# Row maxima of the first and last attention turned by a transposing transfer instead of TensorE: once and twice per batch, written as fp16, with the keys' constant row at minus one

## The reference

```python
# block 0
h = _ln(x) * (1 + sc_msa) + sh_msa
x = x + _self_attn(h) * g_msa           # windows of 128 rows, rolled by 64       -> group "w"
h = _ln(x) * (1 + sc_mca) + sh_mca
x = x + _topk_cross_attn(h, ctx) * g_mca  # top 16 of 256 keys                    -> group "t"
h = _ln(x) * (1 + sc_mlp) + sh_mlp
x = x + _swiglu(h) * g_mlp              # hidden size 1024
# block 1
scores = einsum('bqhd,bkhd->bhqk', q, k) / sqrt(16)
x = x + (einsum('bhqk,bhkd->bqhd', softmax(scores), v) @ Wp + bp)  # 256 x 256    -> group "l"
```

## Time and profile before

| | us |
|---|---|
| median of 3 runs | 1281.58 |
| the profiled execution: its own time | 1281.51 |
| its span, first to last instruction | 1279.6 |
| PE busy (matmul, ends modelled) | 1197.1 |
| DVE busy | 1128.0 |
| ACT busy | 1035.5 |
| POOL busy | 852.7 |
| granted TensorE clock, mean | 0.988 |

### The profile page before, as it was taken

The page is one execution under the profiler, slowest core; times in us unless marked ns, Lnnn a source line. Parts: engine busy times, 40 slices in busy tenths (PEclk is TensorE's granted clock), DMA queues, the critical chain, the costliest instruction groups (busy, mean ns, idle before and its releaser), DMA issues. The chain is left out here.

```text
span 1279.6 us, 39100 instructions
## 1 busy us (share of the span) xinstructions
PE 1197.1 (94%) x13710; PEld 850.3 (66%) x13710; DVE 1128.0 (88%) x3808; ACT 1035.5 (81%) x2193; POOL 852.7 (67%) x1134
## 2 busy tenths in 40 slices
PE   7778898999999999999999999999999999989887
PEld 6665566667676776767676766767676766656654
DVE  3579999899999999999999999999999999988443
ACT  3745688889897979889897989889797979776864
POOL 1315597959586877868686877968596877857310
PEclk9989999999999999999999999999999999999999
DMA  7531021211111121212021121212021121110111
GB/s 200 157 81 43 23 76 34 61 38 45 48 50 54 47 64 27 55 44 73 27 68 44 47 64 52 51 27 64 15 81 30 47 56 42 28 27 2 43 35 34
DMA packets 111392, 67.27 MB, mean 53 GB/s; under 512 B 13836, under 2 KB 107870, under 8 KB 111198
## 3 DMA queue, kind: packets, MB, share of 16 engines
q1 hardware_dynamic: 109166, 63.71, 18.8%
q10 hardware_dynamic: 2032, 1.05, 0.5%
HBM read 22.33 MB, written 4.19 MB: 21 GB/s over the span
## 5 line engine op out<-in xcount | busy, mean ns | idle before, releaser
L1246 ACT ACTIVATE prob<-turned_score 128x1024 f32<-128x1024 f32 x320 | 325.7, 1018 | 82.8 <-PE turned_score L908 81.2
L1521 POOL TENSOR_TENSOR pair<-full,pair 128x512 f16<-128x512 f32 x182 | 210.6, 1162 | 112.8 <-ACT pair L1201 106.6
L1405 DVE MATCH_REPLACE8 rest<-top,score 128x256 f32<-128x256 f32 x512 | 208.2, 415 | 0.0
L1419 DVE MATCH_REPLACE8 far<-best,rest 128x256 bf16<-128x256 f32 x512 | 205.7, 409 | 0.5 <-issue 0.5
L1402 DVE MAX8 top<-score 128x8 f32<-128x256 f32 x512 | 193.4, 419 | 10.7 <-PE score L908 10.3
L1527 POOL TENSOR_SCALAR far<-far 128x512 bf16<-128x512 bf16 x256 | 158.6, 620 | 61.9 <-DVE far L1419 42.6
L1392 DVE TENSOR_REDUCE rowmax_l<-score 128x4 f32<-128x1024 f32 x121 | 147.6, 1220 | 30.5 <-issue 19.8
L908 PE MATMUL work<-pair_n,w_m_hi 128*128 128x256 f16 x1024 | 173.6, 273 | 0.3 <-issue 0.3
L908 PE MATMUL work<-pair_n,w_m_lo 128*128 128x256 f16 x512 | 139.5, 273 | 0.0
L1201 ACT ACTIVATE pair<-full 128x512 f16<-128x512 f32 x192 | 121.0, 630 | 18.0 <-ACT full L1194 0.7
L908 PEld LDWEIGHTS work<-pair_n,w_m_hi 128*128 128x128 f16 x1024 | 96.2, 98 | 20.0 <-issue 9.5
(11 more groups left out here) (212 smaller groups left out, 3191.0 us busy)
## 6 DMA issues: line engine op xcount, KB each, us to landing
k_stack_t<-pair SPq DMA_DIRECT2D x96, 64.0 KB, 2.5
k_stack_l<-pair SPq DMA_DIRECT2D x96, 64.0 KB, 2.6
q_stack_w<-pair SPq DMA_DIRECT2D x93, 64.0 KB, 2.6
k_stack_w<-pair SPq DMA_DIRECT2D x93, 64.0 KB, 2.6
q_stack_t<-pair SPq DMA_DIRECT2D x93, 64.0 KB, 2.6
q_stack_l<-pair SPq DMA_DIRECT2D x93, 64.0 KB, 2.6
ctx_t<-in_ctx_turned SPq DMA_DIRECT2D x16, 256.0 KB, 2.9
ctx_l<-in_ctx SPq DMA_DIRECT2D x16, 256.0 KB, 2.8
```

The source lines that it names most:

```text
L1246: act.activation(prob[:, at:at + 2, :], both_b[:, :, :], ACT.Exp).then_inc(exp_done, 1)
L1405: m = dve.match_replace(rest[p % 2][:, t, :], eight[:, t, :], bank[:, t * L:(t + 1) * L], -FAR)
L1419: m = dve.match_replace(far[p % NFAR][:, t, :], best[p % 2][:, t, :], rest[p % 2][:, t, :], -FAR)
L1521: pool.tensor_tensor(pr[:, 1, :, :], whole[:, :, :], pr[:, 0, :, :], ALU.subtract).then_inc(split_lo, 1)
```

## The change

Groups w and l get their guards another way, except the first batch of w and the last batch of l, which keep the old way (`EDGE_GUARDS`). `rm` writes its maxima as fp16 into a 128x128 tile `rowmax_*`, zeroed once at the start by POOL; w has one such tile, filled by all 4 `rm` of a batch, l has two, each filled by 4 of 8. A new SP piece `gx` waits for the last of these `rm`, turns the whole tile with a transposing transfer from SBUF to SBUF (`turned_max_*`), and `gg`, waiting for it, sends the used rows into the query stack: 32 rows once for w, 16 rows twice for l. `gd` (PE) and `gc` (ACT) go. The top-16 group keeps its four guards per batch.

The maxima are no longer negated by ACT. Instead the keys' constant row is minus one. The same tile of constants multiplied the last projection's bias, so that bias is negated too.

Counts over the whole program: PE's `gd` falls from 192 to 72, ACT's `gc` likewise; SP has 45 `gx` more, and `gg` falls from 192 to 117. All five order lists and the places of the idle matmuls are written anew; the idle matmuls go from 518 to 627.

```diff
+GUARDS = {"w": 1, "t": 4, "l": 2}
+EDGE_GUARDS = {("w", 0): 4, ("l", 15): 4}
...
-IDLE_WORK = ("pj_wq:0:0=59 a_w:0:0=6 gd_w:0:0=22 gd_w:0:1=19 gd_w:0:2=11 bk_w:0:0=17 x4_n2:0:0=25 pj_tq:0:0=38 "
...
+IDLE_WORK = ("pj_wq:0:0=59 wp:0:6=14 gd_w:0:0=19 gd_w:0:2=11 pr_w:0:0=37 x4_n2:0:0=11 pj_tq:0:0=38 a_w:1:0=21 "
...
-        rowmax = {s: [sb(f"rowmax_{s}{i}", [P, 8], F32) for i in range(2)] for s in "wl"}
-        guard = {s: [sb(f"guard_{s}{i}", [8, P], F16) for i in range(2)] for s in "wtl"}
+        edge_rowmax = [sb(f"edge_rowmax{i}", [P, 8], F32) for i in range(2)]
+        rowmax = {s: [sb(f"rowmax_{s}{i}", [P, P], F16) for i in range(GUARDS[s])] for s in "wl"}
+        turned_max = {s: sb(f"turned_max_{s}", [P, P], F16) for s in "wl"}
...
+                elif kind == "gx":
+                    each = (8 if s == "w" else 16) // groups(s, b)
+                    sp.wait_ge(a_free, a_unit(s, b, each * (i + 1) - 1))
+                    if guard_no(s, b, i) > 0:
+                        sp.wait_ge(guard_in[s], 16 * guard_no(s, b, i))
+                    sp.dma_start(turned_max[s][:, :], rowmax[s][i][:, :], transpose=True).then_inc(rowmax_turned[s], 16)
+                elif kind == "gg" and by_transfer(s, b):
+                    many = H // 2 // groups(s, b)
+                    sp.wait_ge(rowmax_turned[s], 16 * (turned_no(s, b, i) + 1))
+                    sp.dma_start(stack[s][b % NS[s]]["q"][NR:64 + NR + 1:64, many * i:many * (i + 1), :],
+                                 turned_max[s][0:4 * many, :]).then_inc(guard_in[s], 16)
...
-                    pe.wait_ge(guard_in[s], 16 * (NG * b + (i if s == "w" else i // 2) + 1))
+                    pe.wait_ge(guard_in[s], 16 * (guard_no(s, b, i * groups(s, b) // (4 if s == "w" else 8)) + 1))
...
-            dve.memset(ones[:, :], 1.0).then_inc(ones_set, 1)
+            dve.memset(minus_ones[:, :], -1.0).then_inc(ones_set, 1)
...
+                    if by_transfer(s, b):
+                        dve.wait_ge(rowmax_zeroed, 1)
+                        if i % each == 0 and turned_no(s, b, g) >= GUARDS[s]:
+                            dve.wait_ge(rowmax_turned[s], 16 * (turned_no(s, b, g) - GUARDS[s] + 1))
+                        maxima = rowmax[s][g]
...
             pool.memset(minus_half[:, :], -0.5)
+            for s in "wl":
+                for one in rowmax[s]:
+                    m = pool.memset(one[:, :], 0.0)
+            m.then_inc(rowmax_zeroed, 1)
```

More of the change, by code:

```diff
@@ L54, with groups, by_transfer, turned_no @@
 BY_TWO = {"wk": 0, "wq": 0, "tq": 0, "lq": 15}
+GUARDS = {"w": 1, "t": 4, "l": 2}
+EDGE_GUARDS = {("w", 0): 4, ("l", 15): 4}
+def groups(s, b):
+    return EDGE_GUARDS.get((s, b), GUARDS[s])
+def by_transfer(s, b):
+    return s != "t" and (s, b) not in EDGE_GUARDS
+def turned_no(s, b, g):
+    return sum(groups(s, one) for one in range(b) if by_transfer(s, one)) + g
+def guard_no(s, b, g):
+    return sum(groups(s, one) for one in range(b)) + g
 ORDERS = {
     "pe": (
[129 rows of a table removed]
-    "act": (
[100 rows of a table removed]
-    "dve": (
[70 rows of a table removed]
-    "pool": (
[88 rows of a table removed]
-}
-IDLE_WORK = ("pj_wq:0:0=59 a_w:0:0=6 gd_w:0:0=22 gd_w:0:1=19 gd_w:0:2=11 bk_w:0:0=17 x4_n2:0:0=25 pj_tq:0:0=38 "
-             "a_w:1:0=13 a_t:0:0=20 b_w:1:0=28 o_w:1:0=8 a_t:0:2=9 a_t:0:5=61 x4_n2:1:0=14 b_t:0:4=16 a_t:1:0=11 "
-             "pr_w:2:0=12 x4_n4:14:0=5 o_l:13:2=12 ot_l:13:0=10 bk_l:13:0=8 m2:15:2=11 x4_n4:15:0=5 pj_lq:15:0=19 "
-             "a_l:15:7=12 bk_l:15:0=14 pr_l:15:0=33")
[118 rows of a table added]
+    "act": (
[89 rows of a table added]
+    "dve": (
[70 rows of a table added]
+    "pool": (
[85 rows of a table added]
+}
+IDLE_WORK = ("pj_wq:0:0=59 wp:0:6=14 gd_w:0:0=19 gd_w:0:2=11 pr_w:0:0=37 x4_n2:0:0=11 pj_tq:0:0=38 a_w:1:0=21 "
+             "a_t:0:0=20 a_w:1:2=14 a_w:1:3=32 a_t:0:1=25 a_t:0:2=11 gd_t:0:0=26 bk_w:1:0=28 pr_w:1:0=22 "
+             "x4_n2:1:0=43 a_t:0:7=5 o_t:0:3=6 bk_t:0:0=19 b_w:2:0=17 pr_w:2:0=5 x4_n3:15:0=43 xt_m:15:0=8 "
+             "x4_n4:15:0=10 a_l:14:7=19 a_l:15:1=10 o_l:14:3=7 bk_l:15:0=14 pr_l:15:0=33")
 def idle_work():
@@ L538, in build @@
         half_bias = sb("half_bias", [P, HC], F32)
-        ones = sb("ones", [33, L], F16)
+        minus_ones = sb("minus_ones", [33, L], F16)
         last_bias = sb("last_bias", [33, C], F16)
@@ L668, in build @@
         guard_out = {s: sem(f"guard_out_{s}") for s in "wtl"}
+        rowmax_zeroed = sem("rowmax_zeroed")
+        rowmax_turned = {s: sem(f"rowmax_turned_{s}") for s in "wl"}
         stat_done = {s: sem(f"stat_{s}") for s in LN if s not in SUMMED}
@@ L757, in unit, with guard_before @@
             return i // 2, i % 2
+        def guard_before(n, s):
+            b = max(one for one in range(B) if guard_no(s, one, 0) <= n)
+            return d_no["gd_" + s, b, n - guard_no(s, b, 0)]
         def heads(g):
@@ L850, in _ @@
                             for one in stack[group]:
-                                sp.dma_start(one["k"][NR:64 + NR + 1:64, :, :], ones[0:H, :]).then_inc(filled, 16)
+                                sp.dma_start(one["k"][NR:64 + NR + 1:64, :, :], minus_ones[0:H, :]).then_inc(filled, 16)
                     if load_no[i] >= NSTAGE:
@@ L1012, in _ @@
                     else:
-                        src = rowmax[s][n % 2][:, :]
-                    turn(d_take(piece, b, i)[0:8, 0:P], src).then_inc(d_ready, 1)
+                        src = edge_rowmax[n % 2][:, 0:rows]
+                    turn(d_take(piece, b, i)[0:rows, 0:P], src).then_inc(d_ready, 1)
                 elif kind == "b":
@@ L1098, in _ @@
                                        k == 0 and n == 0, False)
-                            m = mm(bank[:, t * C:(t + 1) * C], ones[:, 0:P], last_bias[:, :], False, True)
+                            m = mm(bank[:, t * C:(t + 1) * C], minus_ones[:, 0:P], last_bias[:, :], False, True)
                         m.then_inc(d_ready, 1)
@@ L1234, in _ @@
                         act.wait_ge(guard_in[s], 16 * (n - 1))
-                    act.activation(guard[s][n % 2][:, :], d_bank("gd_" + s, b, i)[0:8, 0:P], ACT.Copy,
-                                   scale=-1.0).then_inc(guard_out[s], 1)
+                    act.activation(guard[s][n % 2][0:rows, :], d_bank("gd_" + s, b, i)[0:rows, 0:P], ACT.Copy).then_inc(guard_out[s], 1)
                 elif kind == "e":
@@ L1377, in _ @@
                 elif kind == "rm":
-                    n = NG * b + (i if s == "w" else i // 2)
+                    each = (4 if s == "w" else 8) // groups(s, b)
+                    g, n, half = i // each, guard_no(s, b, i // each), H // groups(s, b)
                     if (s, b, i) not in by_bank_no:
                         dve.wait_ge(a_ready, a_no["a_" + s, b, i])
-                    if n >= 2 and (s == "w" or i % 2 == 0):
-                        dve.wait_ge(d_ready, d_no["gd_" + s, (n - 2) // NG, (n - 2) % NG])
-                    at, wide, of = (0, 4, P) if s == "w" else (2 * (i % 2), 2, L)
+                    if by_transfer(s, b):
[3 more added lines that the diff above has]
+                        maxima = rowmax[s][g]
+                    else:
+                        if i % each == 0 and g >= 2:
+                            dve.wait_ge(d_ready, d_no["gd_" + s, b, g - 2])
+                        maxima = edge_rowmax[n % 2]
+                    at, wide, of = (4 * (i % each), 4, P) if s == "w" else (2 * (i % each), 2, L)
                     if (s, b, i) in by_bank_no:
```

30 lines of the change are left out of this document (16 added, 14 removed), and 747 rows, old and new, of the table ORDERS.

## The result

The changed kernel takes 1304.95 us (median of 4 runs, 1300.71 to 1308.24), the kernel before 1282.62 beside it. The ratio is 1.018 with a 95% interval of 1.016 to 1.020. I had predicted 1271 us and a range of 1257 to 1292. Sign and range are both wrong.

A forecast was written before the change was run, and what follows sets the result against it. The prediction took DVE and PE to share the limit, with PE's list giving way. Turns -19.2, lateness of w +4.5 and DVE order +4.4 made -10.3 us against 1281.51, so 1271 us, range 1257 to 1292.

The forecast's parts named there:

- turns: On PE, 120 turns of w and l go at 0.16 us each: 19.2 us won, counted in full.
- guard of w late: On PE at w's first turned piece: transfers take 5.3 us against 5.0 of cover, 15 times, 4.5 us lost.
- order of DVE: On DVE, 50 places instead of 42 where it waits for PE to refill score banks: 4.4 us lost.
- A microsecond that leaves it lets DVE start that much earlier: Steady stretch: time taken off PE's list passes to DVE in full, until 22.5 us of DVE's waits are used up.
- It is covered: New wait of l: 16 to 24 us of PE matmuls in batches 0 to 11 cover the 5.3 us chain; no cost.
- I count nothing for SP: On SP, 75 guard transfers go, 45 transposing ones come, SP standing still for their landing: counted as no cost.
- rival 4: SP, standing still 45 times for 3 us, delivers top-16 guards late: 13 us against 10.3 won, 1285 us; chance 0.05.
- 1: Rival: the transposing transfer outlasts its cover at PE's first turned piece of w, 15 batches: 1298 us; chance 0.22.
- 2: Rival: DVE is the bound and no PE time passes through: 1279 to 1284 us; chance 0.14.
- 3: Rival: all goes through, 25 us from turns, 5 from PE's waits for maxima, no lateness: 1256 us; chance 0.14.

The follow-up runs named there:

- e5: Kernel before, old lists, without the guards of w and l except in their edge batches, maxima not subtracted there: 1271.8 us, ratio 0.991.
- e15: Kernel before with each of the 120 turns of w and l made three times in a row into the same bank: 1298.2 us, ratio 1.012.
- after: The changed kernel itself, with new lists and transposing transfers for the guards of w and l, against the kernel before: 1304.95 us, ratio 1.018.
- e13: Changed kernel without the guards of w from batch 1 on, l keeping its 30 transposing transfers: 1303.4 us, ratio 1.017.
- e14: Changed kernel with SyncE's list alone changed: l's first transposing transfer and its guard stand behind the key and query transfers, 10 batches: 1326.1 us.
- e6: Changed kernel, new lists, without the guards of w and l except in their edge batches, maxima not subtracted there: 1297.9 us, ratio 1.012 to the kernel before.
- e18: Changed kernel with VectorE's list alone changed at 15 places: l's fourth reduce (4 batches) and w's normalisation (11) one t2 unit later: 1319.5 us.
- e7: Kernel before, old lists, each of the 120 turns and copies of w and l replaced by a transposing transfer on SyncE: 1367.7 us, ratio 1.066.
- before: The kernel without the change, old lists, guards of w and l turned by TensorE, four each per batch: 1282.4 us, 1282.62 beside the changed kernel.

## Why the prediction was wrong, point by point

The sum was -19.2 (turns) + 4.5 (guard of w late) + 4.4 (order of DVE) = -10.3. The runs have -10.6 for leaving out the old guards, +7.0 for the new ones and +26.1 for the lists. So the first term was 8.6 us too good, the second 2.5 too small, and the term of the order 21.7 too small, together 32.8, the whole distance from -10.3 to +22.5. The step that failed is the order term.

**"A microsecond that leaves it lets DVE start that much earlier": wrong by about half.** This was the first step. I took VectorE's 22.5 us of waits for TensorE as room for the whole 19.2. The room was larger than that, since two more rows of 8.7 and 5.5 are waits for scores too, so it was not room that was lacking. e5 and e15 put the share that passes at about 55%, with wide intervals (40 to 87% and 42 to 68%). VectorE's idle time falls from 41.5 to only 38.5 us when all turns are gone. My reading, which no run tests by itself: a wait for a score ends when its matmuls are made after the bank came free, and a shorter list ahead shortens only that part of it in which TensorE came from other work.

**The wait of w: the cover right, both transfers taken too long.** I took 3.2 us for the transposing transfer and 2.1 for the guard behind it, 5.3 against a cover of 5.0, so 4.5 us of lateness in all. In the trace of after the first takes 2.2 us at the median and the second 1.7; the guard has landed 4.0 us after the end of the last reduce (3.9 to 5.4), the first turned piece starts 4.9 to 6.5 us after it (10.6 in batch 15), and in none of the 15 batches does TensorE wait. The 2.1 was misread from the earlier trace rows: the first of its two steps, from 767.08 to 769.71, waited for ACT's copy and not for a landing; only the second, 1.57 us, was one. The term's true value by these rows is nothing. The e13 interval does not exclude that the guard of w costs something by another way.

**"It is covered" and "I count nothing for SP": wrong.** The guards of l are covered, TensorE never waits for them, and yet the guards cost 7.0 us together, most of it with l by the medians. e14 shows one way, in a worse order: the transfer holds SyncE for 1.1 us of issue and, where its guard stands right behind, for some 1.1 us of standing still, and a guard of the top-16 group that queues behind both comes late. That the same happens in after is not shown: TensorE waits 0.6 us for those guards there. I had named this as rival 4, with 3 us of standing still 45 times, 0.05 and 13 us; in after SyncE stands 28.0 us for the 45 landings (17.1 + 10.9), and all guards together cost 7 us. Its argument against, that SyncE stood 175 us for the top-16 guards anyway, compared a sum with something that depends on the moment: SyncE has time to spare on average and, as e14 shows, none where a top-16 guard follows.

**"The order of DVE": this is the step that failed.** I counted 42 and 50 bare places (places where two readers of the score banks follow each other on VectorE with nothing between) and took 0.55 us for each of 8 more: 4.4 us. The order of the other four lists I put at nothing, without a reason. The lists cost 26.1. The count is right by the lists, but it left out three things.
- A bare place has no fixed price. VectorE's and TensorE's rows of e6 around one that is new (start, us, instruction, idle before and released by):

```profile
753.85 1.23 DVE L1420 TENSOR_REDUCE rowmax_l<-score 128x4 f16<-128x1024 f32 x1
756.07 1.23 DVE L1420 TENSOR_REDUCE rowmax_l<-score 128x4 f16<-128x1024 f32 x1 [1.00 <-PE score L930]
...
758.65 1.21 DVE L1420 TENSOR_REDUCE rowmax_l<-score 128x4 f16<-128x1024 f32 x1
760.82 0.37 DVE L1480 RECIPROCAL recip<-work 128x16 f32<-128x16 f32 x2 [0.96 <-PE work L927]
```

```profile
754.17 0.38 PE L930 MATMUL work<-pair_n,w_m_hi 128*128 128x256 f16 x2
...
755.37 0.27 PE L930 MATMUL work<-pair_n,w_m_lo 128*128 128x256 f16 x1
755.58 0.39 PE L930 MATMUL score<-k_stack_l,q_stack_l 48*128 48x256 f16 x4
...
758.31 0.39 PE L930 MATMUL work<-pair,w_q_hi 128*128 128x256 f16 x2
...
759.63 1.09 PE L927 MATMUL work<-ident,osum_l 128*128 128x128 f32 x8
```

  The banks are free at 755.08. TensorE is in the 12 matmuls of an MLP piece until 755.5 and only then makes the scores; VectorE starts at 756.07. About half of its 1.00 us (755.58 to 756.07) is the refill itself, half is what stands ahead on TensorE. Then the outputs of l stand behind 12 projection matmuls (758.31) and VectorE waits 0.96 us ahead of the normalisation. I had looked at neighbours on VectorE alone.
- Places of normalisation (`nv_w`, `nv_l`) are bare places too. They were not in my count and carry 5.0 of the 13.0 us that VectorE's idle time grew between e5 and e6.
- The start. The new lists come to batch 1 some 7 us later than the old, and I had compared the two only for batches in the steady part.

**The rivals.** 1 is refuted by the 2.2 us and by no wait for the guard of w. 2 (no pass-through, 1279 to 1284) and my forecast (all passes) lie on the two sides of what e5 and e15 show; its sign, TensorE idle and VectorE no busier, is what the trace has, but for another reason, the lists. 3 is refuted by e5: without any guard the old lists reach 1271.8, not 1256. 4 is real in e14 and too small by itself. No rival had the cost of the new lists in it, although the diff showed that all five were written anew.

**What stays open.** That the lists carry the loss is shown, and so is the split into start and rest. Which of their moves carries the 1.3 to 1.6 us per batch is not, nor what of it the grouping forces: of VectorE's new idle time some was at the places that e18 repaired, and the repair cost 15 us. Moving the pieces of w and l back as a block was not tried. No version here beats the kernel before with the guards in it; e5, which leaves them out, puts what a cheaper guard could win in the old lists at 10.6 us at most (7.7 to 16.7 by its interval).

## What to carry to other kernels

When a change rewrites the order of work together with an operation, price the two apart: two kernels that leave the operation out, one in each order, told here that the order was worth +26 us and the operation -11 to +7. Where two engines are over 90% busy and feed each other through one pair of banks, don't count in full what is taken off one of them (about half passed here), and before moving a piece read on both engines who is queued behind it: one place can cost more than it frees. A transfer that its own issuing queue must wait for costs that queue issue and landing, so look at what stands behind it and not at the queue's idle time in sum.

## What the runs showed of the hardware

- A transposing transfer of a 128x128 fp16 tile from SBUF to SBUF holds SyncE's queue for 1.1 us of issue, where a plain guard holds it for 0.55, and lands 2.2 to 2.3 us after the start of its issue at the median, where a plain transfer of 64 KB, twice its bytes, takes 2.6. The Trainium skill ("Advanced Engine Details and Errata", section "X-Bar Transpose (TRN2)") has it as fast as a plain one: the landing agrees, as far as transfers of different size can tell, the issue does not. By the Trainium skill, "VectorE: DVE Perf Modes", section "The three transpose paths", the crossbar takes 1309 ns and TensorE 390 ns for a 128x128 tile. No row here isolates the 1309. TensorE's turn of 8 columns costs its list 0.11 us ahead of another turn (e15) and 0.15 to 0.18 ahead of other matmuls (before).
- Its price is not in its own duration: the guards by 45 of them cost 7 us in lists made for them, and a kernel with 120 of them in the old lists, one `turned_max` tile per group, takes 85 us more than the kernel before (e7), with the median landing unchanged.
